# Scores and output products with their two operands 64 bytes apart modulo 128

## The reference

```python
h = layernorm(x, ln1)
x = attention(h, h,   sa_wq, sa_wk, sa_wv, sa_wo, sa_bo) + x     # self attention
h = layernorm(x, ln2)
x = attention(h, ctx, ca_wq, ca_wk, ca_wv, ca_wo, ca_bo) + x     # cross attention
h = layernorm(x, ln3)
a, gate = split(h @ ff_w1 + ff_b1)                               # 1024 columns each
out = (a * gelu(gate)) @ ff_w2 + ff_b2 + x

def attention(xq, xkv, wq, wk, wv, wo, bo):
    q, k, v = heads(xq @ wq), heads(xkv @ wk), heads(xkv @ wv)
    return merge(softmax(q @ k.T / 8) @ v) @ wo + bo
```

## The kernel before

| Tensor | start before | modulo 128 | start after | modulo 128 |
|---|---|---|---|---|
| `w_hi`, `w_lo` | 16512, 49280 | 0 | same | 0 |
| `hT_hi`, `hT_lo` | 133184, 137280 | 64 | same | 64 |
| `qk_hi`, `qk_lo`: queries | 141376, 149568 | 64 | 141376, 150080 | 64 |
| keys (1024 bytes on; now 1088) | 142400, 150592 | 64 | 142464, 151168 | 0 |
| `v_f` | 157760 | 64 | 158784 | 64 |
| `pT` | 190720 | 0 | 191744 | 0 |
| `a_hi`, `a_lo` | 207104, 215296 | 0 | 208192, 216384 | 64 |

## Time and profile before

### The profile page before, as it was taken

The page is one execution under the profiler, slowest core; times in us unless marked ns, Lnnn a source line. Parts: engine busy times, 40 slices in busy tenths (PEclk is TensorE's granted clock), DMA queues, the critical chain, the costliest instruction groups (busy, mean ns, idle before and its releaser), DMA issues.

```text
span 2932.9 us, 76346 instructions
## 1 busy us (share of the span) xinstructions
PE 2880.7 (98%) x25278; PEld 2510.3 (86%) x25278; DVE 2278.4 (78%) x3495; ACT 1911.4 (65%) x6041; POOL 1472.5 (50%) x1310
## 2 busy tenths in 40 slices
PE   8999999999999999999999999999999999999999
PEld 7878888888888888887888888888888889999999
DVE  6878888888888888887888888888888865555554
ACT  6667766666666677876777777777777754444443
POOL 5444444444444444754555555555555545455454
PEclk9999999999999999999999999999999999999999
DMA  5665555555555555566656656666665532222222
GB/s 145 168 170 155 149 149 149 149 149 150 147 147 149 149 149 149 152 164 175 166 159 159 161 159 161 161 161 162 161 162 160 152 109 72 86 75 73 88 72 62
DMA packets 535575, 413.37 MB, mean 141 GB/s; under 512 B 171201, under 2 KB 520769, under 8 KB 535489
## 3 DMA queue, kind: packets, MB, share of 16 engines
q1 hardware_dynamic: 443424, 328.31, 41.1%
q10 hardware_dynamic: 92064, 83.96, 11.2%
HBM read 94.52 MB, written 49.02 MB: 49 GB/s over the span
## 4 chain that ended last, share of the span: by engine, by line
PE 58%; SPq 14%; ACT 12%; DVE 8%; issue 5%; ACTq 3%; DMA 1%; DVEq 0%; POOL 0%; POOLq 0%
PE unit_ps L592 31%; SPq L522 12%; PE s_ps L592 12%; PE o_ps L617 8%; ACT probs L849 8%; PE s_ps L605 7%; ACTq L865 3%; DVE blocks L1043 3%; DVE neg_max L1029 3%; ACT qk_hi L887 3%; DVE hT_lo L1071 1%; DVE hT_lo L1067 1%; DVE qk_lo L1054 1%; ACT x_n L827 1%; DMA rows_in<-rows_t_dram 1%
## 5 line engine op out<-in xcount | busy, mean ns | idle before, releaser
L1259 POOL TENSOR_TENSOR probs<-probs,row_inv 128x1024 f32<-128x1024 f32 x512 | 967.7, 1895 | 956.8 <-DVE row_inv L1034 956.7
L849 ACT ACTIVATE probs<-s_ps,neg_max 128x256 f32<-128x256 f32 x2048 | 952.8, 491 | 266.2 <-DVE neg_max L1029 265.9
L1029 DVE TENSOR_REDUCE neg_max<-s_ps 128x4 f32<-128x1024 f32 x512 | 615.7, 1203 | 72.0 <-PE s_ps L605 71.4
L1043 DVE STREAM_TRANSPOSE blocks<-probs 128x1024 f32<-128x1024 f32 x512 | 632.4, 1235 | 21.3 <-POOL probs L1259 20.9
L592 PE MATMUL unit_ps<-hT_hi,w_hi 128*128 128x256 f32 x2048 | 572.6, 283 | 2.1 <-DVE hT L1024 1.6
L592 PE MATMUL unit_ps<-hT_hi,w_lo 128*128 128x256 f32 x2048 | 555.4, 277 | 0.0
L617 PE MATMUL o_ps<-pT,v_f 128*64 128x256 f32 x4096 | 501.8, 387 | 5.8 <-DMA pT<-blocks 4.6
L592 PE MATMUL unit_ps<-hT_lo,w_hi 128*128 128x256 f32 x1792 | 497.0, 277 | 0.0
L849 ACT ACTIVATION_READ_ACCUMULATOR probs<-s_ps,neg_max 128x1 f32 x2048 | 450.9, 220 | 0.0
L592 PE MATMUL unit_ps<-w_hi,a_hi 128*128 128x256 f32 x1536 | 438.3, 285 | 1.4 <-POOL a_lo L1274 1.0
L592 PE MATMUL unit_ps<-w_hi,a_lo 128*128 128x256 f32 x1536 | 435.0, 283 | 0.0
(11 more groups left out here) (73 smaller groups left out, 6009.7 us busy)
## 6 DMA issues: line engine op xcount, KB each, us to landing
pT<-blocks SPq DMA_DIRECT2D x3072, 64.0 KB, 2.0
pT<-blocks ACTq DMA_DIRECT2D x1024, 64.0 KB, 2.1
rows_t_dram<-row_blocks SPq DMA_DIRECT2D x91, 256.0 KB, 2.4
rows_in<-rows_t_dram SPq DMA_DIRECT2D x91, 256.0 KB, 2.9
x_res<-in_x_dram SPq DMA_DIRECT2D x32, 256.0 KB, 2.7
x_sa_dram<-x_out SPq DMA_DIRECT2D x32, 256.0 KB, 2.2
x_ln<-x_sa_dram ACTq DMA_DIRECT2D x32, 256.0 KB, 3.2
ctx_in<-in_ctx_dram SPq DMA_DIRECT2D x32, 256.0 KB, 2.8
```

What stands on the lines that cost most here:

```text
L849: op = nc.scalar.activation(probs[:, m % 2, r, :], s_ps[:, m % 2, r // IT, r % IT * S:(r % IT + 1) * S], ACT.Exp, bias=neg_max[:, m % RING ...
L1029: nc.vector.tensor_reduce(neg_max[:, m % RING, :], s_ps[:, m % 2, :, :].rearrange("p h (i j) -> p (h i) j", j=S), AX_X, ALU.max, negate=Tr ...
L1043: nc.vector.transpose(blocks[:, n % 2, m % 2, :, :].rearrange("p b (j r c) -> p r j b c", j=IT, c=BLK), probs[:, m % 2, :, :].rearrange("p ...
L1259: nc.gpsimd.tensor_tensor(probs[:, m % 2, :, :], probs[:, m % 2, :, :], row_inv[:, m % RING, :].unsqueeze(2).broadcast_to([P, ROWS, S]), A ...
```

## The change

Queries and keys of a slot get 16 unused floats (64 bytes) behind each 256, so keys lie 1088 bytes after queries instead of 1024. An unused tensor of 64 bytes stands before `a_hi` and another one behind `a_lo`, so these two lie 64 bytes further modulo 128 and everything behind is where it was modulo 128. No instruction is added, removed or moved. The writes of `qk_hi` and `qk_lo`, and the read of `qk_hi` for the remainder, change from one run of 512 elements to two of 256.

```diff
--- before.py
+++ after.py
@@ -27,6 +27,7 @@
 STEPS = PAIRS // 2
 RING = 4
 BLK = 32
+HALF_LINE = 16
 NB = P // BLK
 ROWS = 2 * IT
 BANKS = 3
@@ -213,8 +214,10 @@
         hT = sb("hT", [P, DK, S])
         hT_hi = sb("hT_hi", [P, 2, DK, S], F32R)
         hT_lo = sb("hT_lo", [P, 2, DK, S], F32R)
-        qk_hi = sb("qk_hi", [P, RING, 2, S], F32R)
-        qk_lo = sb("qk_lo", [P, RING, 2, S], F32R)
+
+
+        qk_hi = sb("qk_hi", [P, RING, 2, S + HALF_LINE], F32R)
+        qk_lo = sb("qk_lo", [P, RING, 2, S + HALF_LINE], F32R)
         v_f = sb("v_f", [P, IT, H, DH])
         probs = sb("probs", [P, 2, ROWS, S])
         neg_max = sb("neg_max", [P, RING, 2 * IT])
@@ -223,8 +226,10 @@
         blocks = sb("blocks", [P, 2, 2, NB, IT * ROWS * BLK])
         pT = sb("pT", [P, 2, 2, NB, IT * ROWS * BLK])
         hid = probs[:, 0, 0:2, :]
+        sb("line_off", [P, HALF_LINE])
         a_hi = sb("a_hi", [P, PAIRS, S], F32R)
         a_lo = sb("a_lo", [P, PAIRS, S], F32R)
+        sb("line_on", [P, HALF_LINE])
         gate = probs[:, 1, 0:2, :]
 
         row_blocks = sb("row_blocks", [P, DK * NB, IT * BLK])
@@ -603,7 +608,7 @@
                     for n, (q, k) in enumerate(((qk_hi, qk_hi), (qk_hi, qk_lo), (qk_lo, qk_hi))):
                         for hd, part in enumerate((LEFT, RIGHT)):
                             last = nc.tensor.matmul(s_ps[:, m % 2, hd, it * S:(it + 1) * S], q[part, r, 0, rows],
-                                                    k[part, r, 1, :], start=n == 0, stop=n == 2)
+                                                    k[part, r, 1, 0:S], start=n == 0, stop=n == 2)
                 last.then_inc(at.s_full, 1)
 
             def attend(b, n, home):
@@ -884,7 +889,7 @@
                 bank = unit_ps[:, bank_of(unit), :]
                 if unit[0] == "qk":
                     act.wait_ge(at.qk_full, b * PAIRS + unit[1] + 1)
-                    nc.scalar.copy(qk_hi[:, unit[1] % RING, :, :],
+                    nc.scalar.copy(qk_hi[:, unit[1] % RING, :, 0:S],
                                    bank.rearrange("p (a s) -> p a s", a=2)).then_inc(at.qk_hi, 1)
                 elif unit[0] == "v":
                     _, c, jt = unit
@@ -1051,9 +1056,9 @@
 
             def qk_remainders(b, m):
                 dve.wait_ge(at.qk_hi, b * PAIRS + m + 1)
-                nc.vector.tensor_tensor(qk_lo[:, m % RING, :, :],
+                nc.vector.tensor_tensor(qk_lo[:, m % RING, :, 0:S],
                                         unit_ps[:, bank_of(("qk", m)), :].rearrange("p (a s) -> p a s", a=2),
-                                        f32(qk_hi[:, m % RING, :, :]), ALU.subtract).then_inc(at.qk_lo, 1)
+                                        f32(qk_hi[:, m % RING, :, 0:S]), ALU.subtract).then_inc(at.qk_lo, 1)
 
             def scale_inputs(b, home):
                 dve.wait_ge(at.x_full, b + 1)
```

## The result

The change makes the kernel slower by half a per cent: 2953.9 us (median of six runs, 2950.9 to 2956.4) against 2939.57 (six runs, 2935.07 to 2945.67), a ratio of 1.0048 with a 95% interval of 1.0038 to 1.0057. The profiled execution took 2950.9 us, with a span of 2949.1, 16.2 us more than before.

What follows compares the result with a forecast made beforehand. PE was taken to bound the first pass and feed-forward fully, the second pass partly. Gains of 14 (first pass), 6 (second) and 5 (feed-forward) sum to 25 us off 2934.7, giving 2910; with run spread 2912 us, range 2888 to 2946.

Steps and rivals of the forecast that it cites:

- Moved tensors: All engines: same instructions, order and waits; slices behind a_lo keep their place modulo 128, so no cost.
- Second pass, 6 us of gain: On the second pass's chain, one step's scores and 24 output-product matmuls save 0.17 us per item, 5.6 us over 32.
- Output product, 113.3 ns: Attention's output product falls from 118.3 to 113.3 ns a matmul, saving 0.23 us per item over 46 pitches.
- The remark that matmuls behind a switch can stay slow: Feed-forward rounds: some matmuls behind a switch of product are still slow, so different halves can be quick but need not be.
- rival B: Only one of the two edits works, scores or output product staying slow: gain 9 to 14 us, 2924; chance 0.17.
- Scores, 115: Pairs of scores fall from 120 to 115 ns, saving 0.22 us per item over 44 pitches.
- Unchanged query-key products: Query-key products in the first pass keep their pitch; listed among the signs that the forecast is right.
- Feed-forward, 5 us: Feed-forward rounds of 2.10 us each save 0.02 us, over 8 rounds and 32 items 5 us; bounds 0 and 15.
- The clash that I named at the switches: Feed-forward: `hidden` to `down` gets a new same-half clash at 64, `down` to `hidden` keeps its own; only a third gained.
- Rival A: The halves do not matter; pitches differ for other reasons, so the time stays at 2935 to 2940 (2937); chance 0.20.
- Rival C: Slower, 2950: moving operand's start counts, quick at 64, slow at 0; pairs of scores rise above 120 ns; chance 0.18.
- The gap in `qk_hi` and `qk_lo`: ACT's evacuation and DVE's remainder write two runs of 256: taken as 0, at most 2.6 us in the second pass.

Runs made afterwards that it cites:

- rows_off: Kernel before with only 128 unused bytes ahead of row_blocks, so row_blocks and rows_in start at 128 modulo 256: 2954.61 us, ratio 1.0048.
- load_off: Kernel before with 128 unused bytes between row_blocks and rows_in, so only the load's target is at 128 modulo 256: 2955.16 us, ratio 1.006.
- values_only: Kernel before with only a_hi and a_lo moved 64 bytes further, rows still at 0 modulo 256: 2930.35 us, ratio 0.9973.
- keys_only: Kernel before with only the gap in qk_hi and qk_lo, rows still at 0 modulo 256: 2945.05 us, ratio 1.0016.
- rows_back: The whole change plus 128 unused bytes behind a_lo, putting row_blocks and rows_in back at 0 modulo 256: 2941.84 us, ratio 1.0002 to before.
- inputs_same: Kernel before with activations hT_hi and hT_lo 64 bytes further, on the same half of 128 bytes as the weights: 2966.15 us, ratio 1.0093.

## Why the prediction was wrong

The time came out 42 us above 2912 and above the range. By stage, forecast and measured: -14 and +5 us up to the second pass, -6 and +14 in it, -5 and -3 in the feed-forward stage.

- *The step that failed first* is "Moved tensors": "Slices behind `a_lo` keep their place modulo 128. Nothing for that." It looked at one modulus, that of the change's own idea, and at matmuls alone. The last two tensors are the ends of DMA transfers, and moved by 128 modulo 256. That cost 14 to 17 us (rows_off, load_off), and it stood on the chain of the second pass, where the load lands just ahead of ACT's `hT`.
- *Second pass, 6 us of gain:* the change lost 14 there. The gain was not to be had without the moved rows either: in values_only the output product behind the query-key product takes 2.61 us for 2.72 in all 32 items, and an item still takes 36.07 us for 36.00. The chain of the earlier trace rows is that of one item; what PE won there went into waits (14.5 us for `qk_lo` in values_only from 1500 to 2280 us, 8.7 before).
- *Output product, 113.3 ns:* right as an ability (113.5 in values_only), wrong in the change (117.8). The remark that matmuls behind a switch can stay slow, and the earlier trace rows, with 117.7 ns for an arrangement that should be quick, were the warning. I put that into rival B, with a half of the gain left. For the output product nearly nothing was left: 46 x 0.5 = 23 ns per item in the first pass, for 230.
- *Scores, 115:* measured 118. Two of five ns, or 0.01 us in each of the four steps, 1.61 for 1.62 us.
- *Unchanged query-key products:* the text took them for unchanged and even listed that as a sign of being right. Behind scores they lost 0.09 us, twice per item, in the change and in keys_only alike, though neither their operands nor their instructions had changed. That outweighs all that was won: an item of the first pass went from 36.96 to 37.08 us where I had 36.5.
- *Feed-forward, 5 us:* 16.72 us per item for 16.80, so 2.6 us. The clash that I named at the switches is there, as rounds that are quick and slow in turn.
- *Rival A* comes near the time of rows_back, 2941.84, by luck: the addresses do matter (inputs_same, values_only), and two effects cancel. *Rival C* had the sign but not the mechanism: the moving operand at 0 and the stationary at 64 is quick in values_only, and pairs of scores did not rise above 120.
- *The gap in `qk_hi` and `qk_lo`*, taken as 0, was right: the cast takes 617 ns for 615 and the remainder 688 for 689.
- A reading was wrong, without weight in the sum: the earlier trace rows list a weight load at 0.19 us. The 0.11 us that I called its length is the distance of two starts.

The three edits by themselves give -10 us (values), +5 (keys) and +14 to +17 (rows), 9 to 12 together; the change costs 14. The intervals of the times, some 3 us each, would hardly tell these apart, but the items do: in the first pass the values alone give -0.25 us per item, the keys alone +0.16, and both together +0.12 in place of -0.09. Behind the slow query-key product the values' gain is not there.

What stays open is why a stretch takes the quick or the slow rhythm. The runs show that with values at 64 the output product has the rhythm of the query-key product ahead of it, and that the keys' place goes with how that one runs behind the scores in the first pass, but not in the second. They do not show what else it takes, whether 128 or 256 is the modulus, or what the two streams do inside a matmul.

## What to carry to other kernels

Unused bytes in front of a tensor move everything allocated behind it. Check the target of each load whose rows are just 256 bytes long against 256 as well, and pad back to it. Measure address edits one by one: here one of three gained, and the other two hid its gain. Where a pitch can have two values with the same operands, a neighbour's quick stretch is no price for the one that is moved.

## What the runs showed of the hardware

- A load of 256 KB in rows of 256 bytes landed after 3.5 or 3.6 us instead of 3.1 or 3.2 with its SBUF target 64 or 128 bytes off a multiple of 256 (second pass, beside other transfers). The store whose source moved by 128 bytes, read in rows of 1024, cost nothing that could be measured.
- The matmuls of 256 columns with a new stationary operand each had steady pitches of 113.5 and 117.8 ns with the operands on different halves of 128 bytes, and 118.4 (output product, before) to 120 ns (query-key product, inputs_same) on the same half. The Trainium skill, SBUF — State Buffer, section Who interferes with whom, has TensorE's two read ports independent and TensorE never waiting on anyone, from which one would expect the addresses to change nothing. inputs_same moves two tensors by 64 bytes and the rest behind them by 256, and takes 1.0093 of the time: the measurement decides. Which read waits for what, no run shows.
- Which of the two a stretch has depends on what ran before it, over more than 40 matmuls (query-key product and output product in the change, 1563.08 to 1568.30 us quick and one item later slow), with the same operands and the same granted clock of 1.00.
